# Full and causal attention: scores one step ahead, value products in halves, a group's end inside the next group

## The chip, the cores and the metric

The kernel runs on one core of a Trainium2 chip. The core has a matrix engine (TensorE, PE in the profile, with its weight loads as PEld), a vector engine (VectorE, DVE), a scalar engine (ScalarE, ACT), GpSimd (POOL) and SyncE (SP), which here only issues transfers. The metric is the time of one execution on the device in microseconds (us).

## The reference

Four layers run one after the other on an input of 4 batches, 1024 tokens and 128 features. The change touches the two attentions, which have 16 heads of 8 features each:

```python
x = L0_attn_x                                     # (4, 1024, 128)
x = _layernorm(x + _L0_attn_ref(x, ...))          # full attention, low-rank projections
x = _layernorm(x + _L0_ffn_ref(x, ...))
x = _layernorm(x + _L1_attn_ref(x, Wq, Wk, Wv))   # causal attention
x = _layernorm(x + _L1_ffn_ref(x, ...))           # six blocks of windowed attention and FFN

# _L0_attn_ref                                    # _L1_attn_ref: the same, and causal
scores = jnp.einsum('bhtd,bhsd->bhts', q, k) * scale
attn = jax.nn.softmax(scores.astype(jnp.float32), axis=-1)
y = jnp.einsum('bhts,bhsd->bhtd', attn, v)
```

## The kernel before

The function `attention` runs twice, with tag a1 (full) and a2 (causal). The 4 batches of 16 heads make 16 groups of 4 heads (`GROUPS`, `GH`). Everything of a group is kept in one of two sets of operands, chosen by `par`: `QS` (queries), `KS` and `KZ` (keys, in two forms). q and k are split into three bfloat16 pieces that lie on 48 of the 128 rows; three more rows of `QS` hold each query's maximum, which the rows of -1 in `KS` subtract inside the matmul. So a score comes out of TensorE with its maximum already taken off, and ScalarE takes the exponential without more ado. The price is that the maxima of a group must be known before its scores start, and they are computed while the group before runs.

A group's work has two streams.

The **score stream** has 16 steps in the full attention (`NS`; two halves `hq` of 512 queries, eight blocks `kt` of 128 keys) and 12 in the causal one, where blocks beyond the diagonal are left out and those on it are narrower: the widths of its steps are 512, 384, 256, 128, then five times 512, then 384, 256, 128 columns. A step makes the scores of 4 heads as two pairs (`score`, L425 to L439), each into its own two banks of `a_ps`; ScalarE takes the exponential of a pair into `a_probs` (L517); then 4 value products (`weigh`, L441 to L452) add up in `a_po`, 32 rows for each head. In `a_probs` a step has one of two places, so the exponentials of step s wait until the value products of step s-2 are done.

The **maximum stream** belongs to the next group: 64 chunks in the full attention, 48 in the causal one. A chunk is one matmul into one of the two banks of `a_pm` (`max_chunk`, L404 to L417) and one reduction on VectorE (`half_max`, L337 to L341). Chunk k waits until chunk k-2 has been reduced. The order is written out by hand: 5 chunks a step in the full attention, 6 in the causal one (`per_step`), placed two between the score pairs and the others behind them, and then the value products of the step before. Behind the last chunk the maxima are turned (`turn_maxima`, L419), split into three bfloat16 pieces on VectorE (`finish_maxima`, L343), and ScalarE sends them as three rows into `QS` (`rows_of`, L496); the three transfers are issued ahead of the last step's exponentials.

At the end of each half of 512 queries VectorE copies `a_po` into `a_osum` (`keep_out`, L359), TensorE turns it (`turn_out`, L454), and VectorE divides by the sums (`normalise`, L364). For the second half all this stands behind the last step, ahead of the next group.

SP loads the operands of group g+2 with 12 transfers into the set that group g has used, as soon as the last scores of group g are done (L308 and L309). TensorE's stream for group g+1 starts with a wait for that very load (L474), since its first chunks are those of group g+2.

Of the kernel before, what the change touches and what calls it, by code (L numbers as in the profile page):

```python
# [12 lines left out]
F32 = mybir.dt.float32  # L13
# [5 lines left out]
P = 128  # L19
# [19 lines left out]
GH = 4  # L39
# [199 lines left out]
def attention(nc, A, tag, vals, attn, q_parts, k_parts, ident, causal):  # L239

    with ExitStack() as ctx:
# [18 lines left out]
        p_s = ctx.enter_context(nc.psum_tensor(f"{tag}_ps", [P, 2, 2, CH], F32))  # L265
# [3 lines left out]

# [5 lines left out]
        else:  # L275
# [4 lines left out]
        per_step = -(-NC // (NS - 3))  # L280

        operands, stage_ready = sem("operands", 0), sem("stage_ready")
        maxima, max_read = sem("maxima"), sem("max_read")
        m_all, m_turned, m_lead, m_left, m_split, m_stored = (
            sem("m_all"), sem("m_turned"), sem("m_lead"), sem("m_left"), sem("m_split"), sem("m_stored", 0))
        scores, exped, weighted = sem("scores"), sem("exped"), sem("weighted")
        o_kept, o_turned, o_inv, o_stored = sem("o_kept"), sem("o_turned"), sem("o_inv"), sem("o_stored")
        v_ready, consts, cast, zeroed = sem("v_ready"), sem("consts", 0), sem("cast"), sem("zeroed")
        m_part2, m_done2 = sem("m_part2"), sem("m_mid")

        with nc.Block() as block:
# [20 lines left out]
            def _(pool):  # L312

# [4 lines left out]
                with pool.Fori(0, GROUPS // 2) as i:  # L318
                    for par in range(2):
                        g = i * 2 + par  # L320
                        pool.wait_ge(v_ready, 2 + FIRST)
                        pool.wait_ge(weighted, g * NS + FIRST)
                        src = vals[:, ds(i // 2 * TPB, TPB), ds((i % 2) * 2 * GH + par * GH, GH), :]
                        nc.gpsimd.tensor_copy(V[par][:, :, :, 0:HD + 1], src).then_inc(v_ready, 1)  # L324

            @block.vector
            def _(dve):
                nc.vector.memset(QS[:, :, :, :], 0.0).then_inc(zeroed, 1)
                nc.vector.memset(KZ[:, :, :, :], 0.0).then_inc(zeroed, 1)
                nc.vector.memset(mpart[:, :, :, :], NEG).then_inc(zeroed, 1)  # L330
                dve.wait_ge(zeroed, 4 + FIRST)
# [11 lines left out]
                def finish_maxima(g):  # L343
# [9 lines left out]
                    nc.vector.tensor_copy(mrow[:, 1, :], mrest[:, :]).then_inc(m_part2, 1)  # L353
                    dve.wait_ge(m_part2, g + 1 + FIRST)
# [3 lines left out]
                def keep_out(g, half):  # L358
                    u = g * 2 + half  # L359
                    dve.wait_ge(weighted, g * NS + ends[half] + 1 + FIRST)  # L360
                    dve.wait_ge(o_turned, u + FIRST)
                    nc.vector.tensor_copy(osum[:, :], p_o[:, :]).then_inc(o_kept, 1)

                def normalise(g, half, pos):  # L364

# [13 lines left out]
                for k in range(NC):  # L379
                    half_max(k, 0)  # L380
# [1324 lines left out]
```

## Time and profile before

| | us |
|---|---|
| Median of 3 runs | 7332.78 (7332.68 to 7333.12) |
| The profiled execution | 7338.15 |
| Its span in the trace | 7336.3 |
| TensorE matmul busy | 5478.9 (75%) |
| VectorE busy | 4621.9 (63%) |
| ScalarE busy | 3311.9 (45%) |
| GpSimd busy | 2637.1 (36%) |

Rows of the profile give times in microseconds from the span's start and mean durations in ns. The scores of the full attention run from 180 to 1277 us and those of the causal one from 1810 to 2624 us; the windowed layers behind take the rest, from about 2650 us on. L12 is line 12 of the program before. "PEclk" or the granted clock is the TensorE clock as a share of its full 2.4 GHz, so 0.50 is 1.2 GHz. Matmuls overlap: a matmul of 512 columns is shown with 0.38 to 0.39 us but the next one can start after 0.21 to 0.22 us, so distances are read between starts. Some matmul records are missing. A value product in float32 shows as two records, so that the 4 of a step read x8 in the trace.

### The profile page before, as it was taken

Reading aid. Unit: us, or ns where it says so; the run is one execution under the profiler, and the core shown is the slowest. Engines: PE = TensorE matmul, PEld = TensorE weight load, DVE = VectorE, ACT = ScalarE, POOL = GpSimd, SP = SyncE. Lnnn points to the kernel's source line nnn. Section 1 sums busy time; section 2 is a strip of 40 time slices with the busy share of each in tenths; the row PEclk is TensorE's granted clock in tenths of the full one; section 3 lists DMA queues with packets and bytes.
Section 4 is the critical chain, followed back from the end, with each engine's and each line's share of the span. In section 5 each row is a group of like instructions: output and inputs, shape, how many; then the busy total and the mean of one; then the engine's idle time right before and its main releaser. Section 6 shows DMA issues by size and latency. Waiting matters only on the chain. (4 is left out here: it accounts for less than half of the span.)

```text
span 7336.3 us, 228324 instructions
## 1 busy us (share of the span) xinstructions
PE 5478.9 (75%) x94991; PEld 3176.4 (43%) x95226; DVE 4621.9 (63%) x9757; ACT 3311.9 (45%) x6753; POOL 2637.1 (36%) x2351
## 2 busy tenths in 40 slices
PE   5777877454777746888888888888888888888874
PEld 1222222112232214555555555555555555555552
DVE  5666666345555545676676666666666766666764
ACT  1444444121333313555555555555555555555542
POOL 0000000000000005555555555555555555655550
PEclk9999999576898967888888888888888888888885
DMA  3011010002111101001100110011001100110000
GB/s 95 14 20 20 13 20 14 26 0 84 27 20 26 20 8 52 23 23 29 32 23 23 29 32 23 23 29 32 23 23 31 34 23 23 31 29 23 23 19 18
DMA packets 99949, 197.56 MB, mean 27 GB/s; under 512 B 23616, under 2 KB 50048, under 8 KB 99328
## 3 DMA queue, kind: packets, MB, share of 16 engines
q1 hardware_dynamic: 94944, 195.44, 10.3%
q10 hardware_dynamic: 4896, 0.84, 0.1%
q8 instruction: 47, 0.77, 0.0%
q14 instruction: 62, 0.51, 0.0%
HBM read 67.45 MB, written 27.26 MB: 13 GB/s over the span
## 5 line engine op out<-in xcount | busy, mean ns | idle before, releaser
L340 DVE TENSOR_REDUCE a_mpart<-a_pm 128x1 f32<-128x512 f32 (+2 forms) x1904 | 1087.4, 628 | 511.9 <-PE a_pm L412 316.7
L517 ACT ACTIVATE a_probs<-a_ps 128x1024 f32<-128x1024 f32 (+3 forms) x896 | 796.0, 930 | 1123.5 <-PE a_ps L433 856.2
L1219 ACT ACTIVATE w_probs<-w_pa,w_nm,w_rqs 128x64 f32<-128x64 f32 x3072 | 971.2, 415 | 126.3 <-DVE w_nm L1367 124.4
L412 PE MATMUL a_pm<-a_KZ,a_QS 128*128 128x512 bf16 (+3 forms) x1869 | 665.1, 390 | 301.9 <-DVE a_mpart L340 187.7
L1212 ACT ACTIVATE w_sq<-w_pr 128x512 f32<-128x512 f32 x768 | 466.2, 607 | 898.4 <-DVE w_sinb L1355 898.4
L324 POOL COPY a_V<-a_vals 128x288 f32 x32 | 14.5, 452 | 1913.0 <-PE a_po L449 1911.7
L1141 PE MATMUL w_pr<-w_xc,w_w 128*128 128x256 f32 (+1 forms) x1152 | 455.6, 576 | 293.9 <-issue 293.9
L433 PE MATMUL a_ps<-a_QS,a_KS 128*128 128x512 bf16 (+3 forms) x1688 | 514.9, 379 | 140.9 <-DMA a_KS<-k_parts 118.1
L929 POOL TENSOR_TENSOR w_sinb<-w_sinb,w_tabk 128x512 f32<-128x512 f32 x384 | 488.4, 1272 | 283.8 <-DVE w_sinb L1355 283.8
L955 POOL TENSOR_TENSOR w_probs<-w_probs,w_rden 128x512 f32<-128x512 f32 x384 | 392.9, 1044 | 539.0 <-DVE w_rden L1377 539.0
L1355 DVE STREAM_SHUFFLE w_sinb<-w_pr 128x512 f32<-128x512 f32 x768 | 562.6, 733 | 0.0
L412 PEld LDWEIGHTS a_pm<-a_KZ,a_QS 128*128 128x128 bf16 x1904 | 191.5, 101 | 792.7 <-DVE a_mpart L340 626.3
L1101 PE MATMUL w_pa<-w_probsT,w_Vp 32*64 32x32 f32 x24576 | 499.5, 228 | 16.9 <-issue 16.9
L1101 PE MATMUL w_pa<-w_probsT,w_V 32*64 32x32 f32 x24576 | 500.7, 228 | 12.8 <-issue 12.8
L1101 PEld LDWEIGHTS w_pa<-w_probsT,w_Vp 32*64 32x64 f32 x24576 | 484.9, 131 | 38.7 <-issue 38.7
L937 POOL TENSOR_TENSOR w_ksum<-w_cosb,w_sinb 128x512 f32<-128x512 f32 x384 | 487.6, 1270 | 36.4
L937 POOL TENSOR_TENSOR w_qT<-w_cosb,w_sinb 128x512 f32<-128x512 f32 x384 | 487.3, 1269 | 36.3
L929 POOL TENSOR_TENSOR w_sinb<-w_sinb,w_tabq 128x512 f32<-128x512 f32 x384 | 486.9, 1268 | 9.0 <-DVE w_sinb L1355 9.0
L1141 PEld LDWEIGHTS w_pr<-w_xc,w_w 128*128 128x128 f32 (+1 forms) x1152 | 309.8, 278 | 414.7 <-issue 371.2
L1264 ACT COPY w_oT<-w_pa 128x512 f32<-128x512 f32 x384 | 197.1, 599 | 630.2 <-PE w_pa L1101 630.2
L1101 PEld LDWEIGHTS w_pa<-w_probsT,w_V 32*64 32x64 f32 x24576 | 466.7, 132 | 13.6 <-issue 13.6
L449 PE MATMUL a_po<-a_probs,a_V 128*32 128x512 f32 (+3 forms) x3584 | 436.4, 559 | 31.1 <-ACT a_probs L517 31.1
(218 smaller groups left out, 10160.9 us busy)
## 6 DMA issues: line engine op xcount, KB each, us to landing
w_Vp<-w_V SPq DMA_DIRECT2D x192, 384.0 KB, 3.7
w_Vp<-w_V SPq DMA_DIRECT2D x192, 128.0 KB, 3.4
a_QS<-q_parts SPq DMA_DIRECT2D x136, 96.0 KB, 3.4
a_KZ<-k_parts SPq DMA_DIRECT2D x136, 96.0 KB, 3.6
a_KS<-k_parts SPq DMA_DIRECT2D x136, 96.0 KB, 3.7
q_parts<-a1p_part SPq DMA_DIRECT2D x48, 128.0 KB, 1.8
k_parts<-a1p_part SPq DMA_DIRECT2D x48, 128.0 KB, 1.8
q_parts<-a2p_part SPq DMA_DIRECT2D x48, 128.0 KB, 1.8
```

The lines of the kernel that those rows point to most:

```text
L340: nc.vector.reduce_max(mpart[:, h, qt, kc:kc + 1], p_m[:, k % 2, 0:width], AX_X).then_inc(max_read, 1)
L412: mm = nc.tensor.matmul(out, QS[:, par, h, qt * P:(qt + 1) * P], KZ[:, par, h, kc * CH:kc * CH + width], start=True, stop=True)
L433: mm = nc.tensor.matmul(p_s[:, pair, e, c0:CH], KS[:, par, h, kt * P:(kt + 1) * P], QS[:, par, h, q0:(hq + 1) * CH], start=True, stop=True)
L449: mm = nc.tensor.matmul(p_o[32 * h:32 * h + 32, c0:CH], V[par][:, kt, h, :], probs[:, s % 2, h, c0:CH], start=kt == 0, stop=s in ends, ski ...
L517: nc.scalar.activation(probs[:, s % 2, 2 * pair:2 * pair + 2, c0:CH], p_s[:, pair, :, c0:CH], ACT.Exp, scale=SM_SCALE).then_inc(exped, 1)
L929: nc.gpsimd.tensor_tensor(sinb[:, u % 4, :, :], sinb[:, u % 4, :, :], tab[:, 1:2, :].broadcast_to([P, 2, PAIR]), ALU.mult).then_inc(S[f"si ...
L937: nc.gpsimd.tensor_tensor((ksum if u < 4 else qT)[:, b:b + 2, :], cosb[:, u % 4, :, :], sinb[:, u % 4, :, :], ALU.add).then_inc(S[f"add{u} ...
L1101: mm = nc.tensor.matmul(o_of(w)[64 * e:64 * e + 64, b, t, :], (V if blk else Vp)[r, t, f:f + DH], probsT[r, 2 * e + gl, t, c, blk, :], sta ...
L1141: mm = nc.tensor.matmul(F_BANK[bank][0:hi - lo, at, :], w1[:, off + lo:off + hi], xc[:, :], start=True, stop=True)
L1212: nc.scalar.square(sq[:, u, :, :], UNIT_BANK[u][:, :, :]).then_inc(S[f"sq{u}"], 1)
L1219: op = nc.scalar.activation(probs[:, g, t, c, :], s_of(g)[:, t, c, :], ACT.Exp, bias=nm[:, g, t, c:c + 1], scale=scale_of(g)[:, t, c:c + 1])
L1355: nc.vector.stream_shuffle(sinb[:, u % 4, :, :].rearrange("p a f -> p (a f)"), UNIT_BANK[u][:, :, :].rearrange("p a f -> p (a f)"), SWAP). ...
```

## The change

All of it is in `attention`, for both attentions.

- `score(s+1)` is issued in step s, each pair right behind the wait for that pair's exponential of step s (`next_score`). In the last step it is the next group's first score, and that is where TensorE now waits for the three rows (`m_stored`).
- The value products of step s now stand in step s. Where a step is 512 columns wide they are issued in two halves of 256 columns (`part`, `parts`), with a chunk between the halves.
- A step's chunks stand two behind the first score pair, one behind the second, one between the halves, and the rest behind them. Their number for each step comes from the widths (`room`, `need`): 5 in each of the first 13 steps of the full attention as before, but for one step with 4; in the causal one 10, 4, 3, 1, 8, 6, 6, 5, 5 in its first nine steps, where there were 6 in each of the first eight.
- The copy of `a_po` moves from VectorE to ScalarE, between the two exponentials of the step behind a half. Turning and normalising the second half move into steps 1 and 2 of the next group.
- `turn_maxima` now stands behind the value products of its step, and the three transfers of `rows_of` one step earlier on ScalarE, ahead of the exponentials of step `NS - 2`.
- TensorE's wait for the load (`operands`) stands in step 0 behind the first pair's scores. What starts the load is not changed: the last scores of the group.
- GpSimd's copy of a group's values into `V` is issued a group ahead. Two memsets are added at the start of each attention, and TensorE's loop has a hint for its back edge.

The core of the diff:

```diff
-        per_step = -(-NC // (NS - 3))
+        room = [CH - c0 for _, _, c0 in steps[:NS - 3]]
+        need = [width + 64 for *_, width in chunks]
+        first_chunk, done, k = [0], 0, 0
+        for s in range(NS - 3):
+            while k < NC and (done + need[k] / 2) * sum(room) <= sum(need) * sum(room[:s + 1]):
+                done += need[k]
+                k += 1
+            first_chunk.append(k if s < NS - 4 else NC)
+        first_chunk += [NC] * 3
...
 @block.vector
+                nc.vector.memset(osum[:, :], 1.0)
+                nc.vector.memset(p_o[:, :], 1.0).then_inc(ones_set, 1)
...
                         for s in range(NS):
+                            for k in range(first_chunk[s], first_chunk[s + 1]):
+                                half_max(k, g + 1)
+                            if s == 2:
+                                normalise(g * 2 - 1, 1, place((g + (GROUPS - 1)) % GROUPS))
                             if s == ends[0] + 2:
-                                keep_out(g, 0)
...
+                                normalise(g * 2, 0, place(g))
                             if s == NS - 3:
                                 finish_maxima(g + 1)
-                        keep_out(g, 1)
-                        normalise(g, 1, pos)
...
 @block.tensor
+                def next_score(s, g, par, pair):
+                    pe.wait_ge(exped, g * (2 * NS) + (2 * s + pair + 1) + FIRST)
+                    if s < NS - 1:
+                        score(s + 1, g, par, pair)
+                    else:
+                        if pair == 0:
+                            pe.wait_ge(m_stored, (g + 2) * 48)
+                        score(0, g + 1, 1 - par, pair)
...
-                        pe.wait_ge(m_stored, g * 48 + 48)
-                        pe.wait_ge(operands, (g + 2) * (3 * GH * 16))
...
                         for s in range(NS):
+                            todo = list(range(first_chunk[s], first_chunk[s + 1]))
+                            parts = 2 if steps[s][2] == 0 else 1
+                            next_score(s, g, par, 0)
+                            if s == 0:
+                                pe.wait_ge(operands, (g + 2) * (3 * GH * 16))
+                            for k in todo[0:2]:
+                                max_chunk(k, g + 1, 1 - par)
+                            next_score(s, g, par, 1)
+                            for k in todo[2:3]:
+                                max_chunk(k, g + 1, 1 - par)
+                            weigh(s, g, par, 0, parts)
+                            for k in todo[3:4]:
+                                max_chunk(k, g + 1, 1 - par)
+                            if parts == 2:
+                                weigh(s, g, par, 1, parts)
+                            for k in todo[4:]:
+                                max_chunk(k, g + 1, 1 - par)
+                            if s == 1:
+                                turn_out(g * 2 - 1, g + 1)
+                            if s == ends[0] + 1:
+                                turn_out(g * 2, g + 1)
                             if s == NS - 3:
                                 turn_maxima(g + 1)
...
 @block.scalar
+                def keep_out(u, before):
+                    act.wait_ge(weighted, before + 1 + FIRST)
+                    act.wait_ge(o_turned, u + 1 + FIRST)
+                    nc.scalar.copy(osum[:, :], p_o[:, :]).then_inc(o_kept, 1)
...
-                            if s == NS - 1:
+                            if s == NS - 2:
                                 rows_of(1 - par, g + 1)
-                            for pair in range(2):
+                            for pair in range(PAIRED):
+                                if pair == 1 and s == 0:
+                                    keep_out(g * 2 - 1, g * NS)
+                                if pair == 1 and s == ends[0] + 1:
+                                    keep_out(g * 2, g * NS + ends[0] + 1)
```

What stands in a row on TensorE in a middle step of the full attention. `a_ps` are scores, `a_pm` chunks, `a_po` value products; the REGISTER_ALU rows set up waits. Before:

```order
L433 MATMUL a_ps<-a_QS,a_KS 128x512 x2
L407 REGISTER_ALU
L412 MATMUL a_pm<-a_KZ,a_QS 128x512
L407 REGISTER_ALU
L412 MATMUL a_pm<-a_KZ,a_QS 128x512
L407 REGISTER_ALU
L412 MATMUL a_pm<-a_KZ,a_QS 128x512
L449 MATMUL a_po<-a_probs,a_V 32x512 x4
```

And now, from the second score pair of one step to the first of the next:

```order
L432 MATMUL a_ps<-a_QS,a_KS 128x512 x2
L409 REGISTER_ALU
L413 MATMUL a_pm<-a_KZ,a_QS 128x512
L462 MATMUL a_po<-a_probs,a_V 32x256 x4
L409 REGISTER_ALU
L413 MATMUL a_pm<-a_KZ,a_QS 128x512
L462 MATMUL a_po<-a_probs,a_V 32x256 x4
L409 REGISTER_ALU
L413 MATMUL a_pm<-a_KZ,a_QS 128x512
L443 REGISTER_ALU
L432 MATMUL a_ps<-a_QS,a_KS 128x512 x2
```

The last three chunks stood together ahead of the value products; each now has a half of them, or the next scores, between it and its neighbour.

Where the maxima are turned on TensorE (`a_mcol` into `a_pt`), in the first step without chunks, step 13. Before:

```order
L433 MATMUL a_ps<-a_QS,a_KS 128x512 x2
L428 REGISTER_ALU
L433 MATMUL a_ps<-a_QS,a_KS 128x512 x2
L420 REGISTER_ALU
L421 REGISTER_ALU
L423 MATMUL a_pt<-ident,a_mcol 32x128
L449 MATMUL a_po<-a_probs,a_V 32x512 x4
```

And now:

```order
L432 MATMUL a_ps<-a_QS,a_KS 128x512 x2
L443 REGISTER_ALU
L432 MATMUL a_ps<-a_QS,a_KS 128x512 x2
L462 MATMUL a_po<-a_probs,a_V 32x256 x8
L421 REGISTER_ALU
L422 ISA
L424 MATMUL a_pt<-ident,a_mcol 32x128
```

The turning has moved from before a step's value products to behind them, and the scores ahead of it are those of step 14 now, not of step 13.

ScalarE now, from the exponentials of step 13 on (DMA x3 are the three rows):

```order
L549 ACTIVATE a_probs<-a_ps 128x1024
L519 REGISTER_ALU
L522 DMA a_QS<-a_mrow 1x32x128 x3
L545 REGISTER_ALU
L548 REGISTER_ALU
L549 ACTIVATE a_probs<-a_ps 128x1024
```

Before, the same six rows (L498, L500, L513, L516, L517) stood between the exponentials of step 14 and those of step 15, so the transfers have gone ahead of two exponentials.

## Rows read from the trace of the kernel before

**Rows 1.** Windows of both attentions: length, busy us of each engine, PEclk, DMA.
```profile
180.00:1277.00 1097.00, 866.61 (x4160) 236.78 (x4240) 690.00 (x1199) 499.66 (x512) 6.78 (x15) 0.95 0.10 17
...
1805.00:2624.00 819.00, 599.62 (x4185) 245.02 (x4240) 445.51 (x948) 306.63 (x392) 6.78 (x15) 0.90 0.12 22
```

**Rows 2.** Timeline, full attention: start us, us, engine, line, what, xcount, idle before.
```profile
345.94 0.61 PE L433 MATMUL a_ps<-a_QS,a_KS 128*128 128x512 bf16 x2
...
346.38 0.59 PE L412 MATMUL a_pm<-a_KZ,a_QS 128*128 128x512 bf16 x2
...
346.66 1.94 ACT L517 ACTIVATE a_probs<-a_ps 128x1024 f32<-128x1024 f32 x2 [2.18 <-PE a_ps L433]
...
346.80 3.08 DVE L340 TENSOR_REDUCE a_mpart<-a_pm 128x1 f32<-128x512 f32 x5 [1.04 <-PE a_pm L412]
...
347.55 0.39 PE L412 MATMUL a_pm<-a_KZ,a_QS 128*128 128x512 bf16 x1
...
348.74 0.39 PE L412 MATMUL a_pm<-a_KZ,a_QS 128*128 128x512 bf16 x1 [0.21 <-DVE a_mpart L340]
...
349.06 1.07 PE L449 MATMUL a_po<-a_probs,a_V 128*32 128x512 f32 x8
```

**Rows 3.** Timeline, causal attention: value products 256 columns wide, and what follows.
```profile
1928.40 0.64 PE L449 MATMUL a_po<-a_probs,a_V 128*32 128x256 f32 x8
...
1928.97 0.60 PE L433 MATMUL a_ps<-a_QS,a_KS 128*128 128x512 bf16 x2
```

**Rows 4.** Timeline, full attention: turning and normalising a half.
```profile
358.30 0.65 PE L459 MATMUL a_pt<-ident,a_osum 128*128 128x128 f32 x4
...
358.79 0.59 PE L433 MATMUL a_ps<-a_QS,a_KS 128*128 128x512 bf16 x2
...
359.00 0.26 DVE L368 RECIPROCAL a_rsum<-a_pt 128x16 f32<-128x16 f32 x1 [0.87 <-PE a_pt L459]
...
359.92 3.07 DVE L340 TENSOR_REDUCE a_mpart<-a_pm 128x1 f32<-128x512 f32 x5
```

**Rows 5.** Groups by shape, ScalarE, whole span: busy us, mean ns, idle.
```profile
L1264 ACT COPY w_oT<-w_pa 128x512 f32<-128x512 f32 x384 | 197.1, 599 | 630.2 <-PE w_pa L1101 630.2
...
L517 ACT ACTIVATE a_probs<-a_ps 128x512 f32<-128x512 f32 x64 | 36.5, 596 | 53.5 <-PE a_ps L436 53.5
```

**Rows 6.** Timeline, the boundary between two groups of the full attention.
```profile
302.08 1.04 PE L433 MATMUL a_ps<-a_QS,a_KS 128*128 128x512 bf16 x4
...
306.87 0.11 PEld L433 LDWEIGHTS a_ps<-a_QS,a_KS 128*128 128x128 bf16 x2 [0.43 <-ACT a_probs L517]
...
317.05 1.03 PE L433 MATMUL a_ps<-a_QS,a_KS 128*128 128x512 bf16 x2 [5.03 <-DMA a_KS<-k_parts]
```

**Rows 7.** Timeline: maxima turned, split and sent as rows, start of causal attention.
```profile
1804.77 0.40 PE L468 MATMUL a_pt<-ident,a_mcol 128*32 128x128 f32 x1 [1.04 <-DVE a_mcol L345]
...
1806.39 1.82 ACTq L500 DMA_DIRECT2D a_QS<-a_mrow  x3
```

**Rows 8.** Windows after restarts: TensorE's clock is the number after POOL's count.
```profile
320.00:321.00 1.00, 0.49 (x2) 0.00 (x1) 0.74 (x2) 0.85 (x1) 0.00 (x0) 0.90 0.00 0
...
1916.00:1918.00 2.00, 2.00 (x15) 1.42 (x13) 1.06 (x3) 1.54 (x2) 0.00 (x0) 0.59 0.00 0
```

**Rows 9.** Timeline, POOL: one copy per group, in each attention.
```profile
242.52 0.45 POOL L324 COPY a_V<-a_vals 128x288 f32 x1 [137.53 <-PE a_po L449]
...
1205.71 0.45 POOL L324 COPY a_V<-a_vals 128x288 f32 x1 [68.30 <-PE a_po L449]
...
1905.18 0.45 POOL L324 COPY a_V<-a_vals 128x288 f32 x1 [50.84 <-PE a_po L449]
...
2570.74 0.45 POOL L324 COPY a_V<-a_vals 128x288 f32 x1 [50.76 <-PE a_po L449]
```

**Rows 10.** Timeline, PE, causal attention: a group's first scores, its ninth step's.
```profile
1912.32 0.61 PE L433 MATMUL a_ps<-a_QS,a_KS 128*128 128x512 bf16 x1 [6.10 <-DMA a_KS<-k_parts]
...
1947.58 0.39 PE L433 MATMUL a_ps<-a_QS,a_KS 128*128 128x512 bf16 x1
```

More of the change, by code:

```diff
@@ L239, in attention @@
 def attention(nc, A, tag, vals, attn, q_parts, k_parts, ident, causal):
+    PAIRED = 2
     with ExitStack() as ctx:
@@ L312, in _, with copy @@
             def _(pool):
+                def copy(g, par):
+                    src = vals[:, ds(g // 4 * TPB, TPB), ds(g % 4 * GH, GH), :]
+                    nc.gpsimd.tensor_copy(V[par][:, :, :, 0:HD + 1], src).then_inc(v_ready, 1)
                 nc.gpsimd.memset(KS[:, :, :, :], 0.0).then_inc(zeroed, 1)
@@ L317, in _ @@
                 pool.wait_ge(v_ready, 2 + FIRST)
-                with pool.Fori(0, GROUPS // 2) as i:
+                copy(0, 0)
+                copy(1, 1)
+                with pool.Fori(0, GROUPS // 2 - 1) as i:
                     for par in range(2):
                         g = i * 2 + par
[L321 to L324, printed above, removed]
+                        pool.wait_ge(weighted, (g + 1) * NS + 1 + FIRST)
+                        copy(g + 2, par)
             @block.vector
@@ L426, in score @@
                     hq, kt, c0 = steps[s]
-                    pe.wait_ge(exped, (g * (2 * NS) + (2 * s + pair - 1 if s else 0)) + FIRST)
+                    q0 = hq * CH + c0
+                    diag = causal and kt * P >= hq * CH
                     for e in range(2):
                         h = 2 * pair + e
-                        q0 = hq * CH + c0
-                        diag = causal and kt * P >= hq * CH
                         mm = nc.tensor.matmul(p_s[:, pair, e, c0:CH], KS[:, par, h, kt * P:(kt + 1) * P],
                                               QS[:, par, h, q0:(hq + 1) * CH], start=True, stop=True)
-                        if diag:
+                    if diag:
+                        for e in range(2):
                             mm = nc.tensor.matmul(p_s[:, pair, e, c0:c0 + P], cmaskb[:, 0, :],
@@ L468, in _ @@
                 nc.tensor.transpose(rows0, mcol[:, :], ident[:, :]).then_inc(m_turned, 1)
-                with pe.Fori(0, GROUPS // 2) as i:
+                pe.wait_ge(m_stored, 48)
+                for pair in range(PAIRED):
+                    score(0, 0, 0, pair)
+                with nc.Fori(0, GROUPS // 2, engines=bass.OrderedEngineSet([pe.engine]), hint_back_edge=True) as i:
                     for par in range(2):
                         g = i * 2 + par
-                        pe.wait_ge(m_stored, g * 48 + 48)
-                        pe.wait_ge(operands, (g + 2) * (3 * GH * 16))
-                        k = 0
```

94 lines of the change are left out of this document (39 added, 55 removed).

## Prediction

> **What bounds the kernel now.** I read the windows of the two attentions first. No engine is full in either: TensorE is busy 79% of the full attention and VectorE 63% [rows 1]. So what counts is which wait ends last, and that is read from a timeline of one step and from one of the boundary between groups.
>
> The step repeats every 4.12 us (from 345.94 to 358.30 lie three) [rows 2, 4]. VectorE takes its five reductions in 3.08 us and then waits 1.04 us for a chunk; ScalarE needs 1.94 us for two exponentials and waits 2.18 us [rows 2]. The constants are all in that step. A chunk's matmul is followed by its reduction 0.42 us after its start (346.38, 346.80). The next chunk but one starts 0.75 us after that reduction's start (347.55). Reductions follow each other every 0.616 us. A pair of scores or two chunks take TensorE 0.44 us, a chunk 0.22. From a chunk to the value products it is 0.32 us, and they hold TensorE 1.0 us [rows 2]. With these the step is rebuilt: 0.44 of scores, first reduction at 0.86, third chunk at 1.61, fifth at 2.80, value products at 3.12, next step at 4.12. So VectorE is not the bound: the 1.0 us of value products plus the scores stand between the fifth chunk and the next first one, and two banks of `a_pm` can't bridge that.
>
> The boundary takes 14.97 us, from the scores of step 13 (302.08) to the next group's first (317.05), which wait for the load [rows 6]. A group takes 68.8 us in the full attention (14 periods from 242.52 to 1205.71) and 51.2 us in the causal one (13 from 1905.18 to 2570.74) [rows 9]. The rest, 53.8 and 35.3 us [rows 6, 9, 10], is body: the steps with chunks.
>
> **A step of the full attention.** A value product half as wide holds TensorE 0.57 us (1928.40 to 1928.97) [rows 3], so two halves with two changes from bfloat16 cost 1.14 + 0.20 where one cost 1.0 + 0.10. TensorE's own work in a step is then 4 score matmuls and 5 chunks, 9 x 0.22 = 1.98, and 1.34: 3.3 us. But the loop that closes last is longer. From the third chunk to the fifth lie two chunks' changes and two halves: 2 x (0.32 + 0.57) = 1.78. The fifth's reduction comes 0.42 later, and the second chunk of the next step needs it: 0.75. Then 0.22 to the scores, 0.44 for them, and the third chunk again: 1.78 + 0.42 + 0.75 + 0.22 + 0.44 = 3.61. I take 3.6 us, 0.52 less than before. The exponentials no longer wait for their scores on this path.
>
> **What comes back inside the body.** Turning a half costs TensorE 0.49 us (358.30 to 358.79) [rows 4], twice: 1.0, and one of them stood in the body before too. Normalising puts 0.92 us between 359.00 and the next reduction, 0.3 of it a wait [rows 4]; VectorE's slack in a step is now 3.6 - 3.08 = 0.5, but it stands just where the first reduction should start, so I count 0.6 twice: 1.2. The copy on ScalarE is 0.60 us by the same copy in the windowed layers [rows 5]. It waits for the last value products, then the second exponential (1.0 us) starts, and the second score pair waits for that: 0.65 us once. A step of 4 chunks gives 0.2 back. After the restart TensorE runs at 1.2 GHz until about 320.1, 3 us after 317.05 [rows 8], and 5.3 us in the causal attention (below); in the first step there are now value products in such a stretch too: with 4 us of it, 5.4 us for this step against 3.6. From the restart to the scores of step 13: 5.4 + 12 x 3.6 - 0.2 + 1.0 + 1.2 + 0.65 - 0.44 (one score pair is issued ahead of the wait) = 50.8 us against 53.8. The steps save 3.0 us a group.
>
> **The boundary.** Here the change takes it back. Nothing starts the load earlier: it still follows the last score pair, and from that pair's start to the restart it is 10.18 us (306.87 to 317.05) [rows 6]. The question is how far after the scores of step 13 that pair now comes. Before, 4.79 us. Now, step by step from that point: the scores of step 14, 0.88; value products of step 13, 0.10 + 1.14, to 2.1; only then the turning. From the turning to the end of the third transfer's issue it is 3.44 us (1804.77 to 1808.21) [rows 7]: 5.5. ScalarE has been waiting with these transfers ahead of both exponentials of step 14, which take 2 x 0.97 [rows 2] and 0.2 to start: 7.65. Only then can the second score pair of step 15 go, since its banks are being read. Restart at 7.65 + 10.18 = 17.85, against 14.97: 2.9 us later, and about 0.1 more where the clock has fallen. The next group's first exponentials, ScalarE's copy and the last value products all end by about 13, so the load hides them, but it hid the old end of the group too. That is the whole of the gain: 50.8 + 17.95 = 68.75 against 68.8.
>
> **The causal attention.** By the same steps at its own widths, from the restart: 4.6, 3.4, 2.3, 1.4, 6.0, 3.7, 4.7, 4.1, 3.8 us for steps 0 to 8 (turning, normalising and the copy in them) = 34.0 at full clock. The first 5.3 us after the restart at 1912.32 are at 1.2 GHz (0.59 in the window 1916 to 1918) [rows 8, 10]; ten chunks, the scores and value products fall into them, 2.0 more: 36.0, against 35.3. The body saves nothing here, since the narrow steps before were short already. Boundary: scores 0.66, value products of 384 columns 0.88 (between the 0.57 of 256 columns and 1.0 of 512), turning at 1.54, transfers issued at 4.9, exponentials of 0.60 us each [rows 5] to 6.3, a last pair 0.2 us shorter, restart at 6.3 + 9.98 = 16.3, against 15.9 (51.2 - 35.3). Together 52.2 against 51.2: 1 us slower a group.
>
> **The sum.** Full attention: 15 boundaries with nothing gained, the first group -1 (no load to wait for), the end of the last +3: +2. Causal: 15 x 1 = 15, and the first group +4, since its first step now waits for an exponential and its table load before any chunk. Two memsets twice, VectorE about 1 us each time, bounded by zero (they may fill its wait for GpSimd) and by 2: +1. GpSimd's earlier copies hide behind everything and cost nothing. The back edge's hint: at the back edge TensorE waits for the load anyway, nothing. Together +22 us on the profiled execution's 7338.15 (span 7336.3 and 1.85 around it), so 7360. That execution lies 5.4 us above the median of the runs, 7332.78; I forecast 7354 for the median.
>
> **Two rules weighed.** The trace has 512-column matmuls 0.22 us apart at full clock (0.44 for two) [rows 2]. The Trainium skill, TensorE: Matmul & The Clock Gate, section Back-to-back issue gap, gives about 131 ns for such matmuls in a stream with their weight loads. By that rule the three such spacings in the loop would give 0.27 less a step, some 56 us for 208 steps, and the change would be faster. The row is of this kernel and decides; the sum keeps 0.22.
>
> **Rivals.** *Faster, 7275.* The loop is only TensorE's own work, 3.3 us: the 0.75 us from a reduction to the chunk behind it was taken where TensorE stood waiting, and part of it may be gone when it is busy. 0.3 x 13 steps x 16 groups = 62 us, and about 1 us in each causal group, 16: 7354 - 79. It decides from a step of 3.5 us down. Against it: the same constants give the old step to 0.01 us. For it: what VectorE gains in order can also run ahead over several steps. 0.22.
>
> *Slower, 7400.* The granted clock. In the trace it fell to 0.50 in the 5 us wait for the load, and came back after 3 and 5.3 us of work [rows 8]. The change adds a second gap: TensorE is idle from 2.5 to 6.7 us in step 14. If the clock falls there and stays low through the next two steps, every group pays about 1.5 us more: 31 x 1.5 = 46. The Trainium skill, same page, section HAM oscillation, says that a wait for a transfer between short stretches of work halves the clock anew each time; the trace agrees for the wait it has, and no run yet shows the second gap. 0.20.
>
> *The steps don't shorten, 7440.* If halves of value products cost much more than 0.57 us when a chunk stands between them (weights are changed twice as often), a step stays at 4.0: 0.4 x 208 = 83 us more. Only a pair with scores behind it is in the trace [rows 3]. 0.06.
>
> **From this to the numbers.** The forecast case has 0.52, with its own range 7330 to 7380 (0.1 us in 208 steps is 21 us, 0.7 us in 31 boundaries the same). The rivals have 0.22, 0.20 and 0.06. A difference under 0.2% (14.7 us) can't be told from none here; of the forecast case 0.22 lies within that and 0.30 above. Faster 0.22, the same 0.22, slower 0.56. The range for 8 in 10: from 7285 to 7405.
>
> **What would show it.** Right: reductions of a middle step of the full attention start over every 3.6 us with 0.5 us idle; the wait for the load on TensorE stands after the first score pair and is 5 to 6 us; ScalarE is idle some 6 us ahead of step 14, released by the third transfer; the load's first trigger is 8.3 us after the scores of step 13, not 5.4; groups of 68.7 and 52.2 us. Wrong: steps of 3.3 us; a load that starts as early as before; ScalarE not held by the transfers; a clock at 0.50 in step 2.

## The result, and the profile after

The changed kernel takes 7356.01 us (median of 8 runs, 7351.22 to 7359.46) against 7332.73 for the kernel before (8 runs, 7329.63 to 7340.35): ratio 1.0028, 95% interval [1.0018, 1.0037]. It is a little slower, as forecast. The profiled execution has a span of 7354.6 us against 7336.3.

The two attentions, in the windows of [rows 1]:

```profile
180.00:1277.00 1097.00, 897.99 (x6296) 283.27 (x6296) 699.68 (x1170) 527.86 (x545) 6.34 (x14) 0.94 0.10 17
1805.00:2624.00 819.00, 616.36 (x4941) 258.77 (x4941) 431.77 (x904) 321.92 (x419) 6.36 (x14) 0.90 0.13 22
```

TensorE is busier (82% of the full attention instead of 79%) and nothing is won by it. A middle step of the full attention, VectorE's rows of the timeline:

```profile
405.45 0.69 DVE L349 TENSOR_REDUCE a_mpart<-a_pm 128x1 f32<-128x512 f32 x1 [0.18 <-PE a_pm L413]
406.34 2.53 DVE L349 TENSOR_REDUCE a_mpart<-a_pm 128x1 f32<-128x512 f32 x4 [0.20 <-PE a_pm L413]
409.05 0.69 DVE L349 TENSOR_REDUCE a_mpart<-a_pm 128x1 f32<-128x512 f32 x1 [0.18 <-PE a_pm L413]
```

From 405.45 to 409.05 it is 3.60 us, where it was 4.12 [rows 2, 4]; the wait of 1.04 is now two of 0.18 and 0.20. The boundary, from the scores of step 13 to the next group's first chunk, which is called the restart below. ("The scores of step 13" are in both kernels those that TensorE takes up in its step 13; since the change they belong to step 14.)

```profile
371.52 1.03 PE L432 MATMUL a_ps<-a_QS,a_KS 128*128 128x512 bf16 x4
...
373.48 0.28 PE L424 MATMUL a_pt<-ident,a_mcol 128*32 128x128 f32 x1
...
374.99 1.81 ACTq L522 DMA_DIRECT2D a_QS<-a_mrow  x3
...
376.99 1.94 ACT L549 ACTIVATE a_probs<-a_ps 128x1024 f32<-128x1024 f32 x2 [6.24 <-issue]
...
378.07 1.95 PE L432 MATMUL a_ps<-a_QS,a_KS 128*128 128x512 bf16 x4 [4.30 <-ACT a_probs L549]
378.98 0.13 PEld L432 LDWEIGHTS a_ps<-a_QS,a_KS 128*128 128x128 bf16 x2 [0.79 <-ACT a_probs L549]
...
380.05 0.30 SPq L305 DMA_DIRECT2D a_QS<-q_parts  x1
...
385.05 0.42 SPq L307 DMA_DIRECT2D a_KS<-k_parts  x1
...
389.57 0.64 PE L413 MATMUL a_pm<-a_KZ,a_QS 128*128 128x512 bf16 x2 [4.53 <-DMA a_KS<-k_parts]
...
393.96 0.59 PE L432 MATMUL a_ps<-a_QS,a_KS 128*128 128x512 bf16 x2
```

Read it from below: the chunk at 389.57 waits for the load, whose first trigger (380.05) follows the last score pair, which waited 4.30 us for exponentials, which stood 6.24 us behind three transfers of rows on their own engine, which waited for a turning that stands behind value products. 18.05 us in all, where [rows 6] have 14.97. The label "issue" names no releaser for the 6.24; the ACTq row ahead of it shows what ScalarE was held by. The last row is the next step's first score pair, 4.39 us behind the restart.

POOL's copies mark a group's end, as in [rows 9] (before, the fourteenth ones stand at 1136.96 and 2519.53):

```profile
247.97 0.45 POOL L319 COPY a_V<-a_vals 128x288 f32 x1 [142.86 <-PE a_po L462]
...
1136.36 0.45 POOL L319 COPY a_V<-a_vals 128x288 f32 x1 [67.91 <-PE a_po L462]
...
1859.32 0.46 POOL L319 COPY a_V<-a_vals 128x288 f32 x1 [114.29 <-PE a_po L462]
...
2221.10 0.45 POOL L319 COPY a_V<-a_vals 128x288 f32 x1 [50.76 <-PE a_po L462]
2274.92 0.46 POOL L319 COPY a_V<-a_vals 128x288 f32 x1 [53.37 <-PE a_po L462]
2326.61 0.45 POOL L319 COPY a_V<-a_vals 128x288 f32 x1 [51.23 <-PE a_po L462]
...
2534.29 0.45 POOL L319 COPY a_V<-a_vals 128x288 f32 x1 [53.32 <-PE a_po L462]
```

Over 13 periods a group of the full attention takes 68.34 us (68.80 before), one of the causal attention 51.92 (51.20 before). Most causal groups take 51.2 to 51.4, but four of them 52.0 to 53.8, such as the one that ends at 2274.92.

### The profile page after: what moved, and what is told of

Read it like the earlier page. It is cut to its first block and busy times, and to the rows that moved or that the text cites. A ratio compares the mean times of both kernels' runs of the same rounds, so it can differ in the third digit from the quotient of the medians.

```text
span 7354.6 us, 234325 instructions
## 1 busy us (share of the span) xinstructions
PE 5546.6 (75%) x98062; PEld 3244.5 (44%) x98062; DVE 4621.4 (63%) x9701; ACT 3355.3 (46%) x6819; POOL 2636.6 (36%) x2351
## 5 line engine op out<-in xcount | busy, mean ns | idle before, releaser
L349 DVE TENSOR_REDUCE a_mpart<-a_pm 128x1 f32<-128x512 f32 (+2 forms) x1904 | 1136.8, 631 | 757.0 <-PE a_pm L413 441.9
L549 ACT ACTIVATE a_probs<-a_ps 128x1024 f32<-128x1024 f32 (+3 forms) x896 | 814.9, 934 | 1100.8 <-PE a_ps L432 612.4
L413 PE MATMUL a_pm<-a_KZ,a_QS 128*128 128x512 bf16 (+2 forms) x1904 | 697.0, 385 | 336.8 <-DMA a_KS<-k_parts 232.0
L432 PE MATMUL a_ps<-a_QS,a_KS 128*128 128x512 bf16 (+3 forms) x1800 | 533.5, 386 | 171.0 <-ACT a_probs L549 161.7
L462 PE MATMUL a_po<-a_probs,a_V 128*32 128x256 f32 (+2 forms) x6400 | 540.6, 418 | 0.0
```

What stands on the lines that cost most here:

```text
L349: nc.vector.reduce_max(mpart[:, h, qt, kc:kc + 1], p_m[:, k % 2, 0:width], AX_X).then_inc(max_read, 1)
L413: mm = nc.tensor.matmul(p_m[:, k % 2, 0:width], QS[:, par, h, qt * P:(qt + 1) * P], KZ[:, par, h, kc * CH:kc * CH + width], start=True, st ...
L432: mm = nc.tensor.matmul(p_s[:, pair, e, c0:CH], KS[:, par, h, kt * P:(kt + 1) * P], QS[:, par, h, q0:(hq + 1) * CH], start=True, stop=True)
L462: mm = nc.tensor.matmul(p_o[32 * h:32 * h + 32, cols], V[par][:, kt, h, :], probs[:, s % 2, h, cols], start=kt == 0 and part == 0, stop=s ...
L549: nc.scalar.activation(probs[:, s % 2, 2 * pair:2 * pair + 2, c0:CH], p_s[:, pair, :, c0:CH], ACT.Exp, scale=SM_SCALE).then_inc(exped, 1)
```

## The experiments

For each, the ratio to the kernel before that ran beside it, and from its trace the boundary (scores of step 13 to the restart, one of them) and the mean group over the same 13 periods of POOL's copies. The kernel before took 7337.93 to 7344.26 us beside these runs, against 7332.73 beside the changed kernel, so times from different rows are compared by their ratios.

| kernel | ratio, 95% interval | boundary | full group | causal group |
|---|---|---|---|---|
| before | 1 | 14.97 | 68.80 | 51.20 |
| changed | 1.0028 [1.0018, 1.0037] | 18.05 | 68.34 | 51.92 |
| rows late | 0.9808 [0.9792, 0.9825] | 13.15 | 62.42 | 47.08 |
| load split | 0.9801 [0.9785, 0.9818] | 13.01 | 62.85 | 46.24 |
| both | 0.9782 [0.9766, 0.9798] | 11.77 | 60.91 | 47.74 |
| before + load split | 0.9798 [0.9781, 0.9814] | 10.36 | 64.33 | 46.03 |
| turn first | 1.0013 [1.0004, 1.0022] | 17.23 | 68.44 | 51.68 |
| whole products | 1.0001 [0.9992, 1.0010] | 17.97 | 68.44 | 51.34 |
| busy wait | 1.0012 [1.0003, 1.0021] | 17.91 | 68.26 | 51.38 |
| even chunks | 1.0037 [1.0023, 1.0051] | 18.18 | 68.26 | 52.17 |
| both + weigh first | 0.9720 [0.9705, 0.9735] | 10.02 | 59.92 | 46.04 |
| same, rows on SP | 0.9664 [0.9649, 0.9679] | 10.21 | 59.20 | 44.25 |
| same, one transfer | 0.9695 [0.9680, 0.9709] | 9.84 | 59.84 | 44.89 |
| same, whole products | 0.9693 [0.9678, 0.9707] | 10.62 | 60.26 | 44.29 |

**Rows late** (on the changed kernel).

```diff
-                            if s == NS - 2:
+                            if s == NS - 1:
                                 rows_of(1 - par, g + 1)
```

> The changed kernel with the three row transfers back ahead of step NS-1's exponentials instead of step NS-2's; the turning stays. Theory (the transfers hold ScalarE, so the last score pair and with it the load come late): ScalarE's exponentials of step 14 start about 0.5 us after their scores, the last score pair 2.7 us after the scores of step 13 instead of 7.6, the load's first trigger after 3.5 instead of 8.5, restart about 13.0 us after them instead of 18.05; 5 us in each of 31 boundaries, 155 us: about 7200 us. Rival (the load is late for another reason, or another wait takes its place at once, such as the rows' arrival in front of the next group's first scores): restart still 17 to 18 us after step 13's scores, time within 15 us of 7356. Rival on the clock (the gap in step 14 drops the granted clock and the steps behind pay): beyond the 5 us also the steps from 14 to 1 get shorter, 6 us a boundary or more, below 7170.

Measured 7201.23 us. Its boundary:

```profile
297.33 1.03 PE L432 MATMUL a_ps<-a_QS,a_KS 128*128 128x512 bf16 x4
...
300.67 0.30 SPq L305 DMA_DIRECT2D a_QS<-q_parts  x1
300.80 1.83 ACTq L522 DMA_DIRECT2D a_QS<-a_mrow  x3
...
302.82 1.94 ACT L549 ACTIVATE a_probs<-a_ps 128x1024 f32<-128x1024 f32 x2 [2.84 <-issue]
...
305.42 1.89 PE L432 MATMUL a_ps<-a_QS,a_KS 128*128 128x512 bf16 x4 [3.78 <-DMA a_QS<-a_mrow]
...
310.48 0.60 PE L413 MATMUL a_pm<-a_KZ,a_QS 128*128 128x512 bf16 x2 [0.34 <-DMA a_KS<-k_parts]
...
313.66 0.59 PE L432 MATMUL a_ps<-a_QS,a_KS 128*128 128x512 bf16 x2 [0.16 <-DVE a_mpart L349]
```

The granted clock behind this restart, 1.00 in the number after POOL's count:

```profile
312.00:314.00 2.00, 1.84 (x20) 0.69 (x21) 1.62 (x4) 0.66 (x1) 0.00 (x0) 1.00 0.00 0
```

The first trigger comes 3.34 us after the scores of step 13 instead of 8.53, the restart after 13.15. The theory holds to 0.2 us a boundary. But the load is now awaited for 0.34 us only: what ends last beside it is the rows' arrival at 305.42, with two score pairs, value products and an exponential behind it. A group gained 5.9 us, 1.0 more than this boundary. Part of that lies behind the restart: here the clock is back, and the next step's scores come 3.18 us after the restart (310.48 to 313.66), not 4.39. Behind nine of 14 restarts of this trace it is 3.2 to 3.4 us, behind the other five 4.2 to 4.5. With this one line where the kernel before has it, all the rest of the change makes the kernel 1.9% faster than that one, not 0.3% slower. At the next boundary the rows arrive 6.9 us after the scores of step 13 instead of 8.1, and the load is last by far:

```profile
359.91 0.81 PE L432 MATMUL a_ps<-a_QS,a_KS 128*128 128x512 bf16 x3
...
366.77 1.04 PE L432 MATMUL a_ps<-a_QS,a_KS 128*128 128x512 bf16 x4 [2.76 <-DMA a_QS<-a_mrow]
...
372.49 1.03 PE L413 MATMUL a_pm<-a_KZ,a_QS 128*128 128x512 bf16 x2 [3.15 <-DMA a_KS<-k_parts]
```

Either way it comes to 12.6 to 13.2 us. POOL's copy follows the rows there, so from one copy to the next it reads 59.6 and then 66.0 us, while from restart to restart it is 62.0 and 63.2: only the mean over many periods can be used.

**Load split** (on the changed kernel), and the same on the kernel before.

```diff
                     for h in range(GH):
                         sp.dma_start(QS[0:KROWS, par, h, :], qg[g, :, h, :]).then_inc(operands, 16)
-                        sp.dma_start(KZ[0:KROWS, par, h, :], kg[g, :, h, :]).then_inc(operands, 16)
-                        sp.dma_start(KS[0:KROWS, par, h, :], kg[g, :, h, :]).then_inc(operands, 16)
+                    for h in range(GH):
+                        sp.dma_start(KS[0:KROWS, par, h, :], kg[g, :, h, :]).then_inc(ks_in, 16)
...
                 for g in range(2, GROUPS + 1):
+                    sp.wait_ge(maxima, g * NC + FIRST)
+                    load_kz(g % GROUPS, g % 2)
                     sp.wait_ge(scores, 2 * NS * (g - 1) + FIRST)
                     load(g % GROUPS, g % 2)
```

> The changed kernel with the load split by what frees each buffer: KZ a group earlier (its last reader is long done), QS after the last score pair, KS behind it, waited for in step 2 only. 4 transfers stand between the last score pair and the next group's chunks instead of 12. Theory (the boundary is bounded by the load): last needed trigger 1.4 us after the first instead of 5.0, so the wait for the load in front of the first chunk shrinks from 4.5 to about 1 us: 3.5 us in each of 31 boundaries, 109 us, about 7247. Rival (what the group's end does on TensorE and ScalarE ends just as late): at most the 4.5 us seen idle can go, 140 us; if ScalarE's copy and second exponential are what ends last, under 1 us a boundary, above 7325.

> The kernel before with the same split load, nothing else. Theory: its boundary is bounded by the same load, so it gains the same 3.5 us x 31 = 109 us, about 7224, still 20 us ahead of the changed kernel with it. Rival (with the load no longer last, the changed kernel's 3 us shorter bodies show): the gain of before is smaller than that of the changed kernel by tens of us.

Measured 7195.54 and 7194.89 us. Their restarts:

```profile
310.95 0.60 PE L422 MATMUL a_pm<-a_KZ,a_QS 128*128 128x512 bf16 x2
```

```profile
307.12 1.03 PE L442 MATMUL a_ps<-a_QS,a_KS 128*128 128x512 bf16 x2 [0.23 <-DMA a_QS<-q_parts]
```

In the changed kernel the wait for the load is gone at this boundary: 5.0 us off it, where 3.5 were expected and 4.5 set as the most. The other 0.5 lies in matmuls that a low clock had made longer beside the load, where that cost nothing: the next group's four first score matmuls took 1.69 us (381.81) and take 1.06 (308.23), with the clock back earlier. In the kernel before 4.6 us went, and both kernels stand level. That lies between the two expectations of the kernel before: the changed kernel gained some 18 us more (2.27% against 2.02%), just the difference that was between them. Its shorter body (62.85 - 13.01 = 49.8 against 64.33 - 10.36 = 54.0) is mostly paid back by a boundary 2.7 us longer in the full attention, by nothing gained in the causal one, and by its first groups, which end 5 and 9 us later.

**Both.**

> Both edits: rows ahead of step NS-1's exponentials, and the load split. Theory: the two add up while the load stays last: 5.0 + 3.5 = 8.5 us a boundary would put the restart 9.5 us after step 13's scores; the group's own end (rows, two exponentials of step 15, the first of step 0, the copy) is over by about 9 to 10 us, so nearly all of it counts: 8 us x 31 = 250 us, about 7105. Rival (the chain through rows, exponentials, value products takes over at once): no faster than the better of the two alone, 7200.

Measured 7182.27 us, far from the 7105 and near the rival: 13 us below the load split alone in runs beside each other, with ratio intervals that overlap. Expected was a restart 9.5 us after the scores, it stands at 11.77:

```profile
301.91 1.94 ACT L563 ACTIVATE a_probs<-a_ps 128x1024 f32<-128x1024 f32 x2 [2.84 <-issue]
...
304.27 1.89 PE L441 MATMUL a_ps<-a_QS,a_KS 128*128 128x512 bf16 x4 [3.53 <-DMA a_QS<-a_mrow]
...
306.08 1.73 PE L471 MATMUL a_po<-a_probs,a_V 128*32 128x256 f32 x16
...
308.19 0.59 PE L422 MATMUL a_pm<-a_KZ,a_QS 128*128 128x512 bf16 x2
```

The value products of step 15 have their exponentials at 303.85 but stand behind scores that wait for the rows.

**Weigh first, and rows on SP.** On the kernel with both: the turning ahead of step NS-3's value products, and

```diff
+                            if s == NS - 1:
+                                weigh(s, g, par, 0, 1)
                             next_score(s, g, par, 0)
```

then `rows_of` issued by SP between its KZ and QS transfers instead of by ScalarE.

> Built on rows late + load split. Two more edits on TensorE: the turning ahead of step NS-3's value products, and in step NS-1 the value products ahead of the next group's first scores, so that they no longer stand behind the wait for the row transfers (3.5 us of wait seen there). Theory: rows arrive 0.7 us earlier, value products of step 15 run in the wait, and the next chunks start about 2.2 us earlier: 31 x 2.2 = 68 us off 7182, about 7115; a shorter wait may also spare some of the falls of the granted clock. Rival: the load or the last exponentials take over at once: 7175 or above.

> The same as the weigh-first kernel, with the three row transfers issued by SP, ahead of its load, instead of by ScalarE. Theory: ScalarE's exponentials of step 15 no longer wait 1.8 us behind the issues, the rows leave as early as before, the load's first trigger comes 0.5 to 1 us later: chunks 0.5 us earlier a boundary, 15 us less than the weigh-first kernel. Rival: the load is last again, each boundary 1 us longer, 30 us more.

Measured 7138.58 and 7098.45 us. The value products now run in the wait (302.30, boundary 10.02), 44 us gained instead of 68. Rows on SP, expected to bring 15, brought 40:

```profile
295.26 1.77 SPq L318 DMA_DIRECT2D a_QS<-a_mrow  x3
295.70 1.94 ACT L574 ACTIVATE a_probs<-a_ps 128x1024 f32<-128x1024 f32 x2 [0.56 <-PE a_ps L452]
...
297.08 1.98 SPq L306 DMA_DIRECT2D a_QS<-q_parts  x4
297.69 1.06 PE L482 MATMUL a_po<-a_probs,a_V 128*32 128x512 f32 x8 [0.67 <-ACT a_probs L574]
...
302.70 0.60 PE L433 MATMUL a_pm<-a_KZ,a_QS 128*128 128x512 bf16 x2 [1.60 <-DMA a_QS<-q_parts]
```

On the kernel that it is built on, the same exponentials stood 2.13 us and started right behind ScalarE's three issues (298.31 to 300.12):

```profile
300.31 1.94 ACT L566 ACTIVATE a_probs<-a_ps 128x1024 f32<-128x1024 f32 x2 [2.13 <-PE a_po L471]
```

That became 0.56. Most of the gain is in the causal groups (46.04 to 44.25), which the expectation had not worked out apart. This is the fastest kernel of the study, 3.4% below the kernel before and 3.6% below the changed one.

**One transfer, and whole products on it.** QS and KS of a group in one transfer each for four heads; then `parts = 1`.

> Built on the rows-on-SP kernel: QS and KS of a group each in one transfer for all four heads instead of four. TensorE still waited 1.6 us for the last of the four QS transfers there. Theory: the issue of four (2.0 us) shrinks to one (0.4), so QS lands up to 1.3 us earlier: 31 x 1.3 = 40 us less, about 7058. Rival (the transfer's own time goes up as its size does, the issue was not what counted): within 10 us of 7098.

> The same as the one-transfer kernel with whole value products everywhere. Theory: as on the changed kernel, a plain step costs 3.74 instead of 3.60 us, but the first step after a restart and those with a turning cost less; there the two cancelled in the full attention and 10 us were gained in the causal one. With the restart less disturbed by a low clock the halves should come out ahead: 0 to 15 us slower than the one-transfer kernel. Rival: as on the changed kernel, 10 to 20 us faster.

Measured 7114.11 and 7113.59 us. The first is 0.3% slower than with four transfers, some 23 us by the ratios (their intervals end and begin at 0.9679 and 0.9680), which neither expectation had. The DMA rows (queue, count, KB each, median us from issue to landing) of the kernel with one transfer, then of the one with four:

```profile
a_QS<-q_parts SPq DMA_DIRECT2D x34, 384.0 KB, 5.3
```

```profile
a_QS<-q_parts SPq DMA_DIRECT2D x136, 96.0 KB, 2.8
```

What the issue saved, 1.4 us, the transfer took back with 2.5. In the two attentions TensorE waited for QS 24 times, 32.9 us, instead of 7 times, 10.7 us. Whole products make no difference there; 0 to 15 us more and 10 to 20 less were expected.

**Turn first** (on the changed kernel): only the turning ahead of the value products.

> The changed kernel with one edit: the turning of the maxima stands ahead of step NS-3's value products instead of behind them; the transfers stay ahead of step 14's exponentials. Theory: in the full attention the turning can start 0.7 us earlier (the last reduction ends at 372.67, the turning began at 373.48), in the causal one 0.4 us; the transfers, the last score pair and the load all follow it by the same. 0.7 x 16 + 0.4 x 15 = 17 us: about 7340. Rival (the place of the transfers, not of the turning, is the only thing that counts): 7356 within 5 us.

Measured 7353.18 us, 0.15% below the changed kernel by the ratios, 11 us where 17 were expected, but the intervals overlap: that it is faster at all is not shown by the times. In the trace the boundary is 0.8 us shorter. There the place of the transfers is worth 4.9 us a boundary, that of the turning 0.8.

**Whole products** (on the changed kernel).

```diff
-                            parts = 2 if steps[s][2] == 0 else 1
+                            parts = 1
```

> The changed kernel with whole value products in every step, all else as changed (scores a step ahead, chunks in the same places, the last two now behind the whole product). Theory by the closed loop of the prediction: from the third chunk to the last 0.32 + 1.0 + 0.22 = 1.54 instead of 1.78 us, but the fourth chunk's reduction now starts 0.45 us later and the fifth's right behind it, 0.616 apart: 1.3 + 0.42 + 0.62 + 0.75 + 0.22 + 0.44 = 3.77 us a step against 3.60. 0.17 x 13 x 16 = 35 us, and some 6 in the causal attention: about 7397. Rival (TensorE's own work is what counts): 1.98 + 1.1 = 3.1 us busy, steps no longer than 3.6: 7356 or below. Rival (the halves made all of the gain): steps back at 4.1, 7460.

```profile
405.50 3.11 DVE L349 TENSOR_REDUCE a_mpart<-a_pm 128x1 f32<-128x512 f32 x5 [0.61 <-PE a_pm L413]
409.24 1.89 DVE L349 TENSOR_REDUCE a_mpart<-a_pm 128x1 f32<-128x512 f32 x3 [0.63 <-PE a_pm L413]
```

The step is 3.74 us, as the closed loop said to 0.03. The time is not: 7345.78 us, by the ratios 20 below the changed kernel instead of 41 above it. Around the turning in mid-group the halves lose what they gain (from 416.26 to 432.07 it is 15.8 us with halves; with whole products from 416.72 to 431.91, 15.2), so the full groups are the same, 68.3 but for one of 70.2. The causal ones are 0.6 us shorter on the mean, and most of that is that one of the 13 is long (52.6) where the changed kernel has four; whether whole products keep the others short, one trace of each can't tell. So of the 0.52 us that a plain step lost, the halves brought 0.14, and the kernel as a whole gained nothing by them. The other 0.38 is left to the scores a step ahead and the new places of the chunks; no run parts these two.

**Busy wait** (on the changed kernel): ten matmuls whose result nobody reads, ahead of the wait for the load.

> The changed kernel with ten extra 512-column matmuls on TensorE, into a bank of the maxima that nobody reads, in the wait for the load in front of a group's first chunk. They take about 4.3 us at the low clock, and the wait is 4.5 to 5.1 us. Theory of the clock rival (the wait drops the granted clock and the steps behind it pay): the clock is back at 1.0 at or soon after the restart, where the changed kernel has 0.50 for another 4.4 us in the full and about 5 us in the causal attention; about 1.5 us in each of 31 groups, 46 us: about 7310, and steady causal groups of 51.3 us without the ones of 53.8. Rival (steps behind the restart are bound by VectorE and ScalarE, the low clock hardly counts): 7350 to 7365, though the clock reads higher.

Measured 7346.73 us, about 12 below the changed kernel, with intervals that overlap. The test was too weak to decide:

```profile
386.11 2.32 PE L495 MATMUL a_pm<-a_QS,a_cmaskb 128*128 128x512 bf16 x10
...
391.09 1.03 PE L413 MATMUL a_pm<-a_KZ,a_QS 128*128 128x512 bf16 x2 [2.66 <-DMA a_KS<-k_parts]
```

```profile
388.00:390.00 2.00, 0.43 (x2) 0.00 (x0) 0.00 (x0) 0.31 (x1) 0.00 (x0) 1.00 0.83 115
392.00:394.00 2.00, 2.00 (x12) 0.38 (x10) 1.58 (x3) 0.98 (x1) 0.00 (x0) 0.50 0.01 4
```

The clock was at 1.0 when they began, so they took 2.32 us and not 4.3, and 2.66 us of waiting were left. Behind the restart the clock is at 0.50 all the same, and the full groups are as long as before. The causal mean of 51.38 us comes with one long group instead of four.

**Even chunks** (on the changed kernel): `first_chunk` by `(s + 1) * 6` in the causal attention.

> The changed kernel with the maximum chunks spread as before over the steps: in the causal attention 6 in each of steps 0 to 7 and none in step 8, instead of 10, 4, 3, 1, 8, 6, 6, 5, 5; the full attention keeps its 5 a step. Theory (the new spread suits the steps' widths, so taking it back costs): by VectorE's 0.62 us a wide chunk the causal body comes to 35.8 instead of 34.0 us at full clock, with 0.7 us given back since fewer chunks fall into the low clock after the restart: 1.1 x 16 = 18 us slower, about 7374. Rival (ten chunks in the first step sit in the low clock and cost more than the wide steps give): 0.5 us a group faster, about 7348.

Measured 7366.31 us, but its interval holds the changed kernel's ratio: the spread of the chunks can't be told from no difference here. A kernel 8 us faster would stand at 1.0017, just outside it, which speaks against the rival. The causal groups are no shorter without the new spread (52.17), and five of the 13 take more than 52: it is not what makes the long ones.

## Why the prediction was right

Forecast 7354, measured 7356; by the ratio 20.5 us more than before, where 21 were forecast. The mechanism is the one forecast: shorter steps, paid back by a load that starts later. That the number came so close is partly luck, since terms of 1 to 5 us were off and cancel. Term by term:

- **The step**, 3.6 us: 3.60. The rival at 3.3 us, and with it the 7275, is refuted.
- **The boundary of the full attention**, 17.95: 18.05. Load trigger at 8.3 after the scores of step 13: 8.53. Two small errors cancel in it: the last score pair comes 7.46 us after the scores of step 13 (378.98) and not 7.65, and from it to the first trigger it is 1.07 us, where it was 0.64 before (306.87 in [rows 6], and the row below), since the clock is at 0.50 there. The sum had 0.1 for that and it is 0.4. The wait for the load, forecast with 5 to 6 us, is 4.53. Causal, 16.3: 15.94 (1954.03 to 1969.97). That the place of the row transfers causes it, and not a load that is late anyway, is shown by rows late.

```profile
307.51 0.30 SPq L301 DMA_DIRECT2D a_QS<-q_parts  x1
```

- **The full body**, 50.8: 68.34 - 18.05 = 50.3. The term that was mis-sized is the first step, 5.4 us in the sum and 4.96 without the score pair issued ahead of the wait: it is 4.39 (389.57 to 393.96). The low clock lasted about as long as forecast, 4 us, but made the step only 1.2 us longer than the 3.18 that rows late shows at full clock, not 1.8. Turning and normalising near the restart cost 1.4 us over plain steps (from 394.16 to 406.34 lie three, 12.18 against 10.8) where the sum had 1.1; with the copy in mid-group they cost 1.6 where it had 1.75. So the 15 groups gave 7 us that the forecast put at nothing.
- **The causal group**, 52.2: mostly 51.3, mean 51.92. The forecast's 1 us a group came out nearly (0.7), but not by its reason, and that is luck. Most groups lose 0.1 to 0.2; the rest, 8 us over 13 periods, lies in the four long ones. In the long one from 2221.10 the clock is still 0.50 after 12 us, in the shorter one from 2326.61 it is back at 1.0 after 10. The three that take more than 53 us all have 0.50 from 10 to 12 us after the copy, and none of the others does; why the clock stays low longer in these three is open:

```profile
2233.10:2235.10 2.00, 2.00 (x11) 1.34 (x12) 1.27 (x3) 0.24 (x1) 0.00 (x0) 0.50 0.00 0
```

```profile
2336.61:2338.61 2.00, 1.68 (x12) 0.80 (x12) 1.74 (x6) 0.00 (x0) 0.00 (x0) 1.00 0.00 0
```

- **First groups and memsets.** From an attention's first memset to the first marked copy of POOL it takes 5.1 us longer in the full and 7.3 in the causal attention (123.9 against 116.6). The memsets are 1.1 of it each time, 2.2 where the forecast had 1. Without them and without what belongs to the boundary (3.1 us longer in the full one, and the copy 1.4 and 1.8 us nearer to the restart) -0.5 and +4.4 are left, against -1 and +4.
- **The sum.** Memsets apart, the full attention (to the first matmul of the layer behind it, at 1281.47 before and 1280.42 now) gave 2.5 us where the forecast had it lose 2, and the causal one (to 2626.07 and 2641.81) lost 16.5 where it had 19; the memsets took 1.2 more. Another 2 us came outside the attentions, where nothing was changed. The span grew by 18.3 instead of 22, and the median by 23.3 instead of 21: the profiled execution of the kernel before lay 5.4 us above the median, that of the changed one 0.4. The group of the full attention was the largest error (7 us), and it stayed inside the forecast's own range.
- **The clock rival** at 7400 was half right. The gap in step 14 does drop the clock, to 0.50 from 378 to 380:

```profile
378.00:380.00 2.00, 1.93 (x8) 0.32 (x12) 0.00 (x0) 1.71 (x3) 0.00 (x0) 0.50 0.00 0
384.00:386.00 2.00, 1.04 (x14) 0.14 (x6) 0.00 (x0) 1.35 (x2) 0.45 (x1) 1.00 1.08 150
390.00:392.00 2.00, 2.00 (x12) 0.45 (x10) 1.76 (x3) 0.90 (x1) 0.00 (x0) 0.50 0.02 4
```

  It was back at 1.0 by 384, while the load was still under way, so this fall cost only the 0.4 us by which it delays the load's first trigger. The fall in the wait for the load costs 1.2 us a group in the full attention, by the first steps of 4.39 and 3.18 us above; the kernel before had that fall too. The Trainium skill, TensorE: Matmul & The Clock Gate, section HAM oscillation, lets each wait for a transfer halve the clock anew; the trace agrees at 390. At 378 the clock is down behind a wait for exponentials, which stood behind the issue of transfers. What the fall behind the restart costs in the causal attention stays open.
- **A price per instruction.** The rule of the Trainium skill, same page, section Back-to-back issue gap, about 131 ns for a matmul of 512 columns, does not hold here: the step of 3.60 us closes with 0.22 us a matmul.

## What to carry to other kernels

A transfer issued by a compute engine stands in that engine's order. Count the wait for its data and the issue (1.8 us for three) against everything behind it, and ask which buffer that frees and what load waits for the buffer. Moving these three transfers by one step was worth 2% here; the 0.5 us won in each of 208 steps was paid back at the boundaries while they stood wrong.

When a load bounds a boundary, look at what really frees each of its buffers. One that was free a group earlier (KZ), and one that is needed two steps later (KS), were loaded in the same breath as the one that counted.

A closed loop over one steady step forecasts that step to a few hundredths. It doesn't forecast the kernel: the steps beside a restart or a turning did otherwise, and took back what the halves of the value products won in a plain step.

## What the runs showed of the hardware

- Ten 512-column matmuls in 2.3 us did not keep the clock up through the 2.66 us of idling behind them: 1.00 from 388 to 390, 0.50 from 392 to 394.
- The same first step of a group takes 4.39 us where the clock is at 0.50 for some 4 us behind the restart (389.57, changed kernel) and 3.18 us where it is at 1.00 (310.48, rows late).
- One transfer of 384 KB landed 5.3 us after its issue, one of 96 KB in a row of four 2.8 us. Fewer, larger transfers were slower here, although each issue costs SP 0.42 us.
- The same three transfers of 8 KB let TensorE go 6.9 us after the scores of step 13 at one boundary and 8.1 at another, issued at the same place (363.16 and 300.80, 3.3 and 3.5 us after those scores): they landed 1.8 and 2.8 us after the last issue.
